# Attention steps in pairs on TensorE, a second PSUM pair for the tail of the first attention, scores by query block, some sums on ScalarE, one subtraction on GpSimd

## What is computed

```python
# x: (16, 2048, 1024); every core has 2 sequences of 2048 rows
x = x + LN(attn0(LN(x)))   # A: 16 heads of 64, causal, gelu on q and k, low-rank q/k/v
x = x + LN(ffn0(LN(x)))    # B: ternary weights: h = gelu(x @ Wq(W_fc).T); LN(h); h @ Wq(W_proj).T
x = x + LN(attn1(LN(x)))   # C: 16 heads of 64, no mask, spectral filter on q and k
x = x + LN(ffn1(LN(x)))    # D: three routed feed-forward nets give q, k, v of width 1024,
                           #    then softmax(q @ k.T / 32) @ v
# Wq(W): gamma = mean(|W|) + eps; sign(W / gamma) * min(round(|W / gamma|), 1)
```

## Time and profile before

| what | us |
|---|---|
| median of 3 runs (4946.77 to 5389.83) | 4948.01 |
| the profiled execution | 4945.06 |
| its span, slowest core | 4943.5 |
| TensorE busy in it | 4549.8 |
| ScalarE busy | 2494.5 |
| VectorE busy | 2291.2 |
| GpSimd busy | 1112.4 |
| cores' spans | 4922.7 to 4943.5 |

### The profile page before, as it was taken

The page is one execution under the profiler, slowest core; times in us unless marked ns, Lnnn a source line. Parts: engine busy times, 40 slices in busy tenths (PEclk is TensorE's granted clock), DMA queues, the critical chain, the costliest instruction groups (busy, mean ns, idle before and its releaser), DMA issues.

```text
span 4943.5 us, 56754 instructions; the slowest of 8 cores (4922.7 to 4943.5 us)
## 1 busy us (share of the span) xinstructions
PE 4549.8 (92%) x20820; PEld 1770.3 (36%) x20820; DVE 2291.2 (46%) x3857; ACT 2494.5 (50%) x2891; POOL 1112.4 (23%) x1124
## 2 busy tenths in 40 slices
PE   6788879999999999999998899899999999999999
PEld 3222234444422223444443223344442222244444
DVE  5887755544113344344465544555511234343445
ACT  4577743222398886122225787233229988812220
POOL 1067733322111100023010101334321110002300
PEclk9798999999999999999999999999999999999999
DMA  7656554333223322422161122433311112233002
GB/s 189 190 189 192 182 181 147 114 117 97 54 45 82 70 81 63 120 52 44 62 175 43 44 63 92 160 111 118 111 41 31 33 54 79 58 94 88 26 35 94
DMA packets 319034, 471.86 MB, mean 95 GB/s; under 512 B 177902, under 2 KB 217008, under 8 KB 308528
## 3 DMA queue, kind: packets, MB, share of 16 engines
q1 hardware_dynamic: 291248, 427.60, 28.2%
q0 software_dynamic: 27520, 40.64, 5.2%
HBM read 384.00 MB, written 99.09 MB: 98 GB/s over the span
## 4 chain that ended last, share of the span: by engine, by line
PE 76%; DVE 11%; DMA 4%; ACT 3%; issue 3%; POOL 3%; SPq 0%; DVEq 0%; ACTq 0%; POOLq 0%
PE pall L190 75%; ACT arena L201 3%; DVE arena L217 3%; DVE arena L204 2%; DVE arena L214 2%; POOL arena L204 1%; DVE cols L221 1%; DMA arena<-l0f_w2T 1%; POOL arena L208 1%; DVE cols L541 1%; DVE cols L543 1%; DVE arena L720 1%; DMA arena<-l_wkr 1%; DMA arena<-w_scr 1%; DMA arena<-x_in 1%
## 5 line engine op out<-in xcount | busy, mean ns | idle before, releaser
L190 PE MATMUL pall<-arena 128*128 128x512 bf16 (+3 forms) x20668 | 4536.3, 381 | 359.2 <-DVE arena L204 101.6
L190 PEld LDWEIGHTS pall<-arena 128*128 128x128 bf16 (+3 forms) x20668 | 1757.1, 100 | 3130.9 <-issue 1598.7
L201 ACT ACTIVATE arena<-pall,cols 128x1024 bf16<-128x1024 f32 (+3 forms) x2096 | 1968.4, 1010 | 903.7 <-PE pall L190 883.8
L204 DVE TENSOR_TENSOR arena<-arena 128x512 f32<-128x512 f32 (+5 forms) x980 | 659.3, 678 | 825.4 <-ACT arena L201 663.8
L201 ACT ACTIVATE arena<-pall 128x512 bf16<-128x512 f32 (+3 forms) x480 | 312.7, 653 | 1265.8 <-PE pall L190 1260.4
L204 POOL TENSOR_TENSOR arena<-arena 128x512 f32<-128x512 f32 (+1 forms) x472 | 554.3, 1175 | 878.3 <-ACT arena L201 442.6
L204 POOL TENSOR_TENSOR cols<-cols 128x1 f32<-128x1 f32 (+2 forms) x282 | 191.2, 678 | 1763.4 <-DVE cols L208 1530.4
L217 DVE COPY arena<-pall 128x512 f32<-128x512 f32 (+1 forms) x226 | 146.0, 682 | 376.9 <-PE pall L190 376.8
L217 DVE CAST arena<-pall 128x512 bf16<-128x512 f32 (+1 forms) x160 | 118.6, 741 | 413.5 <-PE pall L190 413.5
L217 POOL CAST arena<-arena 64x512 bf16<-64x512 f32 (+1 forms) x136 | 86.1, 633 | 912.7 <-DVE arena L217 733.5
L208 POOL TENSOR_SCALAR arena<-arena,cols 128x512 bf16<-128x512 f32 x128 | 222.8, 1752 | 33.2 <-DMA arena<-l0f_wfcT 16.3
(11 more groups left out here) (58 smaller groups left out, 569.8 us busy)
## 6 DMA issues: line engine op xcount, KB each, us to landing
arena<-wfc_scr SPq DMA_DIRECT2D x64, 1024.0 KB, 5.3
z_scr<-arena SPq DMA_DIRECT2D x96, 512.0 KB, 2.6
arena<-z_scr SPq DMA_DIRECT2D x96, 512.0 KB, 4.0
arena<-x_in SPq DMA_DIRECT2D x64, 512.0 KB, 5.5
arena<-l0f_wfcT SPq DMA_DIRECT2D x64, 512.0 KB, 4.9
arena<-l0f_w2T SPq DMA_DIRECT2D x64, 512.0 KB, 4.5
arena<-wqf_scr SPq DMA_DIRECT2D x64, 256.0 KB, 2.6
arena<-sel_scr SPq DMA_DIRECT2D x32, 512.0 KB, 8.9
```

The lines of the kernel that those rows point to most:

```text
L190: return self.pe.put(lambda e: e.matmul(out, lhsT, rhs, start=start, stop=stop), after, signal)
L201: lambda e: e.activation(out, in_, func, bias=bias, scale=scale), after)
L204: return q.put(lambda e: e.tensor_tensor(out, a, b, op), after)
```

## The change

Five edits.

- **Pairs.** The attention loop goes in steps of two: S(i), exp(i), S(i+1), masks of i-2 and i-1, PV(i-2), exp(i+1), PV(i-1), then two ticks. `emit_s` is split into `emit_s` and `emit_exp`. Buffers stay: two PSUM pairs for scores, three `pt`.
- **A second pair for the tail.** At the start of block B the two banks of `k.ob` are added to `k.xpool`; `take(2)` now wants two neighbouring banks, the lower one even.
- **Scores by query block.** `scores(qb)` waits for the q tiles of its own block (`qblock[qb]`) instead of all.
- **Sums.** Of each 32 sums, every third (10; 20 in all) is an `Abs` activation with accumulation on ScalarE, in place in its load buffer.
- **Subtraction.** `a4` of `post` runs on GpSimd in sequence 0 (16 times).

```diff
     def take(self, n=1, first=False):
         while True:
-            ready = [b for b in self.xpool if b.ready <= self.now]
+            ready = sorted((b for b in self.xpool if b.ready <= self.now),
+                           key=lambda b: b.idx)
+            if n == 2:
+                pairs = [[a, b] for a, b in zip(ready, ready[1:])
+                         if b.idx == a.idx + 1 and a.idx % 2 == 0]
+                ready = pairs[0] if pairs else []
...
-    for i in range(len(steps)):
+
+    for i in range(0, len(steps), 2):
         emit_s(i)
-        if i >= 1 and steps[i - 1][0]:
-            emit_mask(i - 1)
-        if i >= 2:
+        emit_exp(i)
+        emit_s(i + 1)
+        if i:
+            for j in (i - 2, i - 1):
+                if steps[j][0]:
+                    emit_mask(j)
             emit_pv(i - 2)
-        if state["late"]:
-            emit_recip()
-        rs, rb = rate(steps[i][0], i, causal and steps[i][2] >= 4 * steps[i][0])
-        k.tick(0.55 + 0.55 * (512 - steps[i][3]) / 512, rs, rb)
+        emit_exp(i + 1)
+        if i:
+            emit_pv(i - 1)
+        for j in (i, i + 1):
+            if state["late"]:
+                emit_recip()
+            rs, rb = rate(steps[j][0], j, causal and steps[j][2] >= 4 * steps[j][0])
+            k.tick(0.55 + 0.55 * (512 - steps[j][3]) / 512, rs, rb)
...
-        a = k.red(acc[:, i:i + 1], k.f32(QZ_KB + 4 * j, 1024), ALU.add, [tok], absval=True)
+        W = k.f32(QZ_KB + 4 * j, 1024)
+        if i % 3 == 2:
+            a = k.act.put(lambda e, W=W, i=i: e.activation(W, W, AF.Abs,
+                                                         accum_out=acc[:, i:i + 1]), [tok])
+            onact = a
+        else:
+            a = k.red(acc[:, i:i + 1], W, ALU.add, [tok], absval=True)
...
     hb = [k.bank[0], k.bank[1], k.bank[2]]
+    for b in k.ob:
+        b.ready = k.now + 2.0
+        k.xpool.append(b)
...
         outtok[f] += res
+        qblock[g] = res
...
-                           [outtok["k"], outtok["q"], b.free] if dc == 0 else (), dc == 7)
+                           [outtok["k"], qblock[qb], b.free] if dc == 0 else (), dc == 7)
...
-                a4 = k.ts(k.dve, z, z, sc["ve"], None, ALU.subtract, after=[a2, a3])
+                a4 = k.ts(k.gp if seq == 0 else k.dve, z, z, sc["ve"], None, ALU.subtract,
+                          after=[a2, a3])
+                sc["free"] = [a4]
```

More of the change, by code:

```diff
@@ L625, in emit_attention @@
     p_tok = {}
+    s_tok = {}
     def emit_s(i):
@@ L637, in emit_s, with emit_exp @@
         k.last_qk = tok
+        s_tok[i] = tok
+    def emit_exp(i):
+        qb, c, kt, off, last = steps[i]
+        s = sbank[i % 2]
+        tok = s_tok.pop(i)
         j = i % 3
```

5 lines of the change are left out of this document (3 added, 2 removed).

## The result

The changed kernel is slower: 1.0092 times the kernel before, with a 95% interval of 1.0077 to 1.0108, so 46 us on 4948. It took 4985.65 to 4997.43 us, 4992 at the median, where 4911 was forecast and 4985 was the upper end of the range.

What follows compares the result with a forecast made beforehand. Attention steps with inserted matmuls were taken as bound by TensorE, bare ones by ScalarE. Terms +14 - 22 - 20 - 6 - 4 + 1 = -37 us gave 4908 profiled, 4911 at the median, range 4855 to 4985.

Steps and rivals of the forecast that it cites:

- The slot wait: Attention pairs: exp(i+1) waits for PV(i-2), behind S(i+1), which waits for exp(i-1); a bare pair takes 2.23 us.
- The chain of five terms: Bare pair, exp(i-1) to exp(i+1): 1.11 + 0.11 + 0.35 + 0.23 + 0.43 = 2.23 us, where ScalarE alone needs 2.0.
- The rival by which pairs gain everywhere: All attentions: exp(i+1) does not wait for PV(i-2) last, bare pairs bound by ScalarE at 2.0 us; 4791 us, chance 0.12.
- The second attentions: Block C, 255 pairs each: 606 us by pair counts plus 7 of disturbance, 613 us; +7 each, +14 for both.
- and I take the same: First attention of sequence 0: sequence 1's -11 us taken over despite the weights' preparation on VectorE; range -35 to +20.
- The 26 us for narrower scores: First attention of sequence 1, 24 diagonal groups: 0.85 us less exp and some 0.25 less matmul time, -26 us.
- The tail: Block B: loads start 10 us sooner, so TensorE's wait for the `W2` chunks falls to 5 us; -20 for both sequences.
- Scores: Start of D's scores: the 3.40 us wait for the last q tile goes; -3 for each sequence, -6 in all.
- Sums and subtraction: 20 sums moved to ScalarE: -4 us; 16 subtractions on GpSimd at 3.5 us each, delaying stores: +1 us.
- the one that ends slower: Bare attention pairs: late VectorE copies or masks hold up exp(i+1), 0.15 us for each of 520; 4989 us, chance 0.15.
- The clock's rival: Bare attention pairs: TensorE's lower busy share halves the clock for a third of them, costing 139 us; 5050 us, chance 0.04.
- The rival by which the tail brings nothing: Block B: chunk loads still released behind the hidden phase, subtraction and sums cost their bounds; 4936 us, chance 0.09.

Runs made afterwards that it cites:

- The fourth buffer: The changed kernel with four `pt` buffers in place of three, heads scaled wrongly with the same instructions; 0.9989 of the kernel before, 4947 us.
- the experiment with split ticks: The changed kernel with, in sequence 0's first attention, one tick between exp(i) and S(i+1) and masks ahead of their ticks; 1.0051 of the kernel before, 4970 us.
- the pairs alone: The kernel before with the attention loop in pairs and nothing else; 1.0132 of the kernel before, single times 4990, 4997 and 5046 us.
- with 64 rows at partitions 64 to 127: The changed kernel with four `pt` buffers, ticks split in sequence 0's first attention, selection matrix on partitions 64 to 127; 0.996 of the kernel before, 4929 us.

## Why the prediction was wrong, step by step

**The slot wait and its price: right.** The chain of five terms gave 2.23 us, and the trace has 2.23; the doubtful last term of 0.43 measured 0.42. One reading under it was wrong: the exp of 1.19 us was put beside one of 1.11 "where the other engines leave it alone". In the trace of the kernel before, exps with VectorE at work beside them last no longer (1.13 us on average) than those without (1.16); those that begin before the last one has ended last 1.17, the others 1.11. The term of 1.11 stands, by another reason. The fourth buffer brought 2.01 back. The rival by which pairs gain everywhere is out: it describes the kernel only once the buffer is free, and even then not for pairs with inserted matmuls. The rule of the Trainium skill that a change of tiling mode drains TensorE (page "TensorEngine Tiling (Array Packing)", section "Key Properties") agrees with TensorE's busy time, 33 us less in one second attention; that drain is simply not what ends last in a bare pair.

**The second attentions: mechanism right, size short.** +14 forecast, +20 measured. The bare pairs were sized right, 2.23 us at the median. Pairs with six inserted matmuls were taken at 2.81 us and measured 3.13 and 3.09 (means of all cores in the two attentions); with 26 of them that is some 8 us for each attention. Those with four were taken at 2.55 and measured 2.70 and 2.63, 2.85 in the first query block, where they are the q projection. Part of it came back in pairs with none or one, taken at 2.23 and measured 2.16 and 2.07.

**The first attention of sequence 0: "and I take the same".** This is the step that failed: -11 was carried over from sequence 1 by likeness, +20 came, 31 of the 83 us between forecast and measurement. The prediction named VectorE's 334 busy microseconds there and put no price on two portions in a row; the pairs' price in TensorE's and ScalarE's queues was worked out, that in VectorE's was not. The runs show in its place masks that are done up to 2 us later, and the experiment with split ticks gives 24 us back. That VectorE's queue is the whole of it is argued, not shown, as that edit moves the inserted matmuls as well.

**The first attention of sequence 1: mis-sized.** -11 forecast, +1 measured. The 26 us for narrower scores were too much: it makes a diagonal pair 1.68 us on average, and bare diagonal pairs measured 1.9 to 2.1 on average (before 1.9 to 2.0). Why they stay so long was not taken apart; a chain that is shortened in one of its exps still has its waits for masks and its other terms. Besides, the old sum for this stage was never made, so nothing showed that the terms did not add up.

**The tail: right up to the wait that it removes, wrong on what is late next.** The wait for `w_scr` went from 15 to under 3 us, where 5 was forecast; in sequence 1 it had been 12.7 us and not 14.84, which is the length of the load in the chain of the earlier trace rows. The next late thing was said to be nothing ("TensorE's work before the projections is unchanged"); it is the additions of squares on VectorE, behind two chains and not one. -20 forecast, -3 measured.

**Scores: the same fault in small.** The wait that goes is 3.40 us, the one that comes 3.60. "Next late is the matmul of the norms" was written down and priced too low; -6 forecast, +0.6 and +0.2 measured for D, the subtraction included.

**Sums and subtraction.** -4 and +1 forecast. The sums gave nothing that can be told from the spread of the cores (2.3 us more in the changed kernel, 1.7 with the pairs alone, which has no such sums). The subtraction was taken at 3.5 us and took 2.9; nobody waits for it.

Of the rivals, the one that ends slower (the slot wait costs more, at 4989 us) nearly met the number, 4992, but not by its reason: the slot wait cost what it was said to cost. The clock's rival fell: 0.99 in the second attention of sequence 0, with 1.00 before. The rival by which the tail brings nothing was right in its result and not in its reason: the loads did come early, and another wait took the place of theirs.

## What to carry to other kernels

When an order of instructions is changed, write the old and the new order for every engine that is written from the same loop, not only for the two that the change speaks of: here that of VectorE, which the prediction had left out, was worth up to 24 us. Where every engine runs its queue in order, saving work on one helps only if no closed chain of waits through it is longer than its work; and a wait that stands ahead of the inserted work can't be filled by it. And for every wait that a change removes, name the engine that is late next with its own time, and price that, before counting a gain.

## What the hardware showed that I had not expected

A kernel in which 32 matmuls of each attention, among thousands of full ones, contract over 16 rows took 4991 us, and its twin with 128 rows in them 4947. The loss goes with TensorE's clock. In the first attention of sequence 0 the first eight of these matmuls ran at a granted clock of 0.50 on seven of the eight cores, and from the first score to the last the stage took 458.3 us at a mean clock of 0.820, where the twin took 441.0 at 0.867. In that of sequence 1 it was 369.0 us at 0.931 against 357.0 at 0.962 (medians of the cores): length times clock is 343.5 and 343.4 there, and in sequence 0 376 and 382, so the clock can account for the whole loss. Later groups of eight often ran at 1.00, and why only some are hit stays open. The two kernels differ in the number of rows, in where the two operands lie and in the values multiplied; with 64 rows at partitions 64 to 127 the cost was some 20 us or less, so the row count is the likeliest cause, not a shown one.

An absolute-value activation of 128x1024 f32 from SBUF took ScalarE 1.053 us, while GpSimd's subtraction over 128x1024 f32 took 2.899 us, where VectorE needs 0.753.
